# Whole-matrix loads on two queues and a transpose by DMA, in an eight-core attention and FFN layer kernel

## The reference

```python
def attn(x, bind_key, unbind_key, gate, decay):        # x: [8, 2048, 1024]
    bound = circ_conv(x, bind_key)
    d = sigmoid(decay)
    decay_matrix = where(t >= s, d ** (t - s), 0)
    hologram = einsum('ts,bsd->btd', decay_matrix, bound)
    return x + gate * circ_corr(hologram, unbind_key)

def ffn(x, w_gate, w_up, w_down):                      # int weights / 127, hidden 3072
    h = silu(x @ wg.T) * (x @ wu.T)
    return h @ wd.T

x = x + layernorm(attn(layernorm(x)))
x = x + layernorm(ffn(layernorm(x)))
```

## Time and profile before

| | us |
|---|---|
| median of 2 runs | 831.39 (831.27 to 831.5) |
| profiled execution, whole time | 832.75 |
| profiled execution, span of the slowest core | 831.2 |
| spans of the 8 cores | 818.4 to 831.2 |
| PE busy in the span | 679.4 |
| DVE busy, ACT busy | 248.8, 208.2 |

### The profile page before, as it was taken

The page is one execution under the profiler, slowest core; times in us unless marked ns, Lnnn a source line. Parts: engine busy times, 40 slices in busy tenths (PEclk is TensorE's granted clock), DMA queues, the critical chain, the costliest instruction groups (busy, mean ns, idle before and its releaser), DMA issues.

```text
span 831.2 us, 8438 instructions; the slowest of 8 cores (818.4 to 831.2 us)
## 1 busy us (share of the span) xinstructions
PE 679.4 (82%) x3030; PEld 300.2 (36%) x3030; DVE 248.8 (30%) x595; ACT 208.2 (25%) x309; POOL 40.7 (5%) x80
## 2 busy tenths in 40 slices
PE   0538489999700699799999999699999999999994
PEld 0113222343300344344444444343444444444441
DVE  0532431055557212612121123233111111112333
ACT  2001422244341421211111132423111111112222
POOL 7000000000000000000000000000000000000000
PEclk9878765699955599899999999789999999999998
DMA  7999500000002034434444201013444444400111
GB/s 176 237 259 165 93 1 0 1 1 0 1 0 51 1 53 76 76 52 76 76 77 76 50 26 52 25 44 84 76 76 76 77 76 76 76 1 26 51 52 76
DMA packets 13145, 53.40 MB, mean 64 GB/s; under 512 B 1472, under 2 KB 1472, under 8 KB 12848
## 3 DMA queue, kind: packets, MB, share of 16 engines
q0 software_dynamic: 10800, 44.47, 28.7%
q1 hardware_dynamic: 2304, 8.39, 2.5%
HBM read 80.12 MB, written 8.39 MB: 106 GB/s over the span
## 4 chain that ended last, share of the span: by engine, by line
PE 71%; DVE 9%; issue 6%; ACT 6%; DMA 5%; POOL 2%; DVEq 0%; ACTq 0%; POOLq 0%
PE pg L642 20%; PE pu L650 19%; PE pu L719 10%; PE pf L719 10%; DMA x<-xin 5%; PE pb L364 4%; PE cp L239 3%; ACT t1a L439 2%; DVE sqd L418 2%; PE pt L579 2%; ACT t1a L411 2%; PE pb L359 1%; DVE sta L544 1%; DVE x2t L583 1%; PE pr L481 1%
## 5 line engine op out<-in xcount | busy, mean ns | idle before, releaser
L642 PE MATMUL pg<-x2t,wgu 128*128 128x512 bf16 x768 | 178.6, 387 | 9.5 <-DVE xw L669 6.9
L650 PE MATMUL pu<-x2t,wgu 128*128 128x512 bf16 x768 | 173.6, 379 | 0.0
L663 ACT ACTIVATE sil<-pg,z 128x512 bf16<-128x512 f32 x96 | 65.5, 687 | 241.0 <-PE pg L642 240.9
L642 PEld LDWEIGHTS pg<-x2t,wgu 128*128 128x128 bf16 x768 | 76.0, 99 | 104.7 <-issue 18.0
L650 PEld LDWEIGHTS pu<-x2t,wgu 128*128 128x128 bf16 x768 | 75.1, 98 | 90.6
L669 DVE SCALAR_TENSOR_TENSOR xw<-sil,pu 128x512 bf16<-128x512 bf16 x64 | 43.7, 688 | 167.9 <-PE pu L650 165.8
L239 PE MATMUL cp<-cubb,cbtb 128*128 128x512 bf16 x128 | 38.3, 471 | 46.2 <-DMA x<-xin 43.8
L481 PE MATMUL pr<-hc,zt 128*128 128x512 bf16 x256 | 63.1, 391 | 7.5 <-ACT t1a L411 6.6
L719 PE MATMUL pf<-wdtb,xw 128*128 128x512 bf16 x256 | 57.9, 379 | 2.1 <-DVE hc L669 2.1
L719 PE MATMUL pu<-wdtb,xw 128*128 128x512 bf16 x256 | 59.5, 387 | 0.0
L64 POOL DMA_DIRECT2D wgu<-wgu x48 | 25.4, 530 | 679.8 <-PE pu L650 441.9
(11 more groups left out here) (94 smaller groups left out, 450.5 us busy)
## 6 DMA issues: line engine op xcount, KB each, us to landing
wgu<-wgu POOLq DMA_DIRECT2D x48, 512.0 KB, 5.1
x<-xin POOLq DMA_DIRECT2D x16, 512.0 KB, 28.5
out<-x SPq DMA_DIRECT2D x16, 512.0 KB, 2.7
wdtb<-wdt POOLq DMA_DIRECT2D x1, 6144.0 KB, 81.1
cbtb<-cbt POOLq DMA_DIRECT2D x4, 512.0 KB, 23.3
cubb<-cuT POOLq DMA_DIRECT2D x4, 512.0 KB, 25.5
cstf_s<-cstf POOLq DMA_DIRECT2D x1, 257.0 KB, 3.3
cstb_s<-cstb POOLq DMA_DIRECT2D x1, 128.0 KB, 2.9
```

What stands on the lines that cost most here:

```text
L642: pe_g[eta][c] = op("tensor", lambda e, sl=sl, c=c, d=d: e.matmul(PG[sl][:, 512 * c:512 * c + 512], WGU[sl][:, 128 * d:128 * d + 128], X2T ...
L650: pe_u[eta][c] = op("tensor", lambda e, sl=sl, c=c, d=d: e.matmul(PU[sl][:, 512 * c:512 * c + 512], WGU[sl][:, 1024 + 128 * d:1024 + 128 * ...
L663: sc_sil[eta][c] = op("scalar", lambda e, sl=sl, c=c: e.activation(SIL[sl][:, 512 * c:512 * c + 512], PG[sl][:, 512 * c:512 * c + 512], AF ...
```

## The change

Three things change. First, the X tiles are loaded from SP, each 512 KB without a cast, at the very start; POOL loads the two circulants whole, one DMA each, and issues WDTB only after all X tiles have landed. Second, the circulant product waits for both circulants, then goes block by block through 4 PSUM banks, with the contraction index on the inside. Third, X2T is filled by a DMA transpose from SP in place of PE, PT and the DVE copy: ACT's tile tl waits for the transpose of tile tl - 2 (semaphores XA0, XA1, XB0, XB1), and the gate matmuls wait for the last two transposes.

```diff
+    for t in range(TN):
+        dma("sync", X[t][:], xin[:, 1024 * t:1024 * t + 1024], f"LDX{t // 4 + 1}".replace("LDX1", "LDX"))
-    for q in range(4):
-        gsem = f"LDX{q + 1}".replace("LDX1", "LDX")
-        dma("gpsimd", CBTB[:, 2048 * q:2048 * q + 2048], cbt[:, 2048 * q:2048 * q + 2048], gsem)
-        dma("gpsimd", CUBB[:, 2048 * q:2048 * q + 2048], cuT[:, 2048 * q:2048 * q + 2048], gsem)
-        for t in range(4 * q, 4 * q + 4):
-            dma("gpsimd", X[t][:], xin[:, 1024 * t:1024 * t + 1024], gsem)
+    dma("gpsimd", CBTB[:], cbt[:, :], "WCC")
+    wt_ccin = dma("gpsimd", CUBB[:], cuT[:, :], "WCC")
+    for gname in ("LDX", "LDX2", "LDX3", "LDX4"):
+        w("gpsimd", gname, 64)
     wt_wd = dma("gpsimd", WDTB[:], wdt[:, :], "WWD")
...
-    CP = [pa.enter_context(nc.psum_tensor(f"cp{i}", [128, 512], F32)) for i in range(8)]
+    CP = [pa.enter_context(nc.psum_tensor(f"cp{i}", [128, 512], F32)) for i in range(4)]
+    w("tensor", "WCC", wt_ccin)
-    for half in range(2):
-        g0 = 8 * half
-        if half == 1:
-            w("tensor", "SC", dv_ccevac[7])
+    for g in range(16):
+        dj, fc = g // 2, g % 2
+        if g >= 4:
+            w("tensor", "SC", dv_ccevac[g - 4])
         for k in range(ND):
...
-            w("scalar", "PE", pe_tr[tl - 2] if tl >= 2 else prev_pe_tr[tl - 2])
+            if tl >= 2:
+                w("scalar", f"X{HN}{tl % 2}", xt[tl - 2])
+            elif prev_xt is not None:
+                w("scalar", f"XA{tl % 2}", prev_xt[tl + 6])
             sc_x2[tl] = op("scalar", lambda e, t=t, tl=tl: e.activation(
                 X2S[tl % 2][:], X[t][:], AF.Identity,
                 bias=NB2s[:, t:t + 1], scale=R2s[:, t:t + 1]), "SC")
-            for d in range(ND):
-                pe_tr[tl] = op("tensor", lambda e, tl=tl, d=d: e.transpose(
-                    PT[:, 128 * d:128 * d + 128], X2S[tl % 2][:, 128 * d:128 * d + 128], IDB[:]),
-                    "PE" if d == ND - 1 else None)
-            w("vector", "PE", pe_tr[tl])
-            dv_pt[tl] = op("vector", lambda e, tl=tl: e.tensor_copy(...), "DV")
+            w("sync", "SC", sc_x2[tl])
+            if tl == 0:
+                w("sync", "PE", pe_before)
+            sem = f"X{HN}{tl % 2}"
+            plan["sync"].append(lambda e, tl=tl, s=sem: e.dma_start_transpose(
+                X2T[:, :].rearrange("p (d t) -> p d t", d=ND)[:, :, 128 * tl:128 * tl + 128],
+                X2S[tl % 2][:, :].rearrange("p (d t) -> p d t", d=ND)).then_inc(S[s], 16))
```

More of the change, by code:

```diff
@@ L40, in build_nc @@
     C = {"LDX": 0, "LDX2": 0, "LDX3": 0, "LDX4": 0, "LDC": 0, "WCC": 0, "WWD": 0,
-         "WG0": 0, "WG1": 0, "PE": 0, "DV": 0, "SC": 0, "GP": 0, "ST": 0}
+         "WG0": 0, "WG1": 0, "XA0": 0, "XA1": 0, "XB0": 0, "XB1": 0,
+         "PE": 0, "DV": 0, "SC": 0, "GP": 0, "ST": 0}
     S = {}
@@ L170, in finish_debug @@
         w("sync", "PE", C["PE"])
-        for snm in ("WCC", "WWD", "WG0", "WG1"):
+        for snm in ("WCC", "WWD", "WG0", "WG1", "XA0", "XA1", "XB0", "XB1"):
             w("sync", snm, C[snm])
@@ L228, in build_nc @@
     last_chain_end = {0: 0, 1: 0}
-    for half in range(2):
-        g0 = 8 * half
-        if half == 1:
-            w("tensor", "SC", dv_ccevac[7])
+    for g in range(16):
+        dj, fc = g // 2, g % 2
+        if g >= 4:
+            w("tensor", "SC", dv_ccevac[g - 4])
         for k in range(ND):
[L234 to L250, removed]
+            pe_cc[g] = op("tensor", lambda e, dj=dj, fc=fc, k=k, g=g:
+                          e.matmul(CP[g % 4][:], CBTB[:, 1024 * k + 128 * dj:1024 * k + 128 * dj + 128],
+                                   CUBB[:, 1024 * k + 512 * fc:1024 * k + 512 * fc + 512],
+                                   start=(k == 0), stop=(k == ND - 1)),
+                          "PE" if k == ND - 1 else None)
+        w("scalar", "PE", pe_cc[g])
+        dv_ccevac[g] = op("scalar", lambda e, dj=dj, fc=fc, g=g:
+                          e.activation(HC[dj][:, 512 * fc:512 * fc + 512], CP[g % 4][:],
+                                       AF.Identity, bias=0.0, scale=1.0), "SC")
         if phases <= 0.77:
             continue
+        t = g
         if t % 4 == 0:
-            w("vector", f"LDX{t // 4 + 1}".replace("LDX1", "LDX"), 96)
+            w("vector", f"LDX{t // 4 + 1}".replace("LDX1", "LDX"), 64)
         p = 12 * (t % 2)
@@ L557, in emit_ln2, with emit_x2pipe @@
         return ln_combine(tg0, 8, M1c, R2s, NB2s, fold=INV127)
-    def emit_x2pipe(hf, dv_ln2, psum_sc, psum_dv, prev_pe_tr):
+    def emit_x2pipe(hf, dv_ln2, pe_before, prev_xt):
         tg0 = 8 * hf
-        PT = ffps["PT"]
         sc_x2 = [0] * 8
-        pe_tr = [0] * 8
-        dv_pt = [0] * 8
+        xt = [0] * 8
+        HN = "B" if hf else "A"
         for tl in range(8):
@@ L571, in emit_x2pipe @@
                 bias=NB2s[:, t:t + 1], scale=R2s[:, t:t + 1]), "SC")
-            w("tensor", "SC", sc_x2[tl])
+            w("sync", "SC", sc_x2[tl])
             if tl == 0:
[L574 to L577, removed]
-            for d in range(ND):
-                pe_tr[tl] = op("tensor", lambda e, tl=tl, d=d: e.transpose(
-                    PT[:, 128 * d:128 * d + 128], X2S[tl % 2][:, 128 * d:128 * d + 128], IDB[:]),
-                    "PE" if d == ND - 1 else None)
-            w("vector", "PE", pe_tr[tl])
[L583 to L590, removed]
+                w("sync", "PE", pe_before)
+            sem = f"X{HN}{tl % 2}"
+            C[sem] += 16
+            xt[tl] = C[sem]
+            plan["sync"].append(lambda e, tl=tl, s=sem: e.dma_start_transpose(
+                X2T[:, :].rearrange("p (d t) -> p d t", d=ND)[:, :, 128 * tl:128 * tl + 128],
+                X2S[tl % 2][:, :].rearrange("p (d t) -> p d t", d=ND)).then_inc(S[s], 16))
+        return sc_x2, xt
     dv_ln2_done = 0
@@ L599, in build_nc @@
             dv_ln2_done = emit_ln2(0, 0)
+            _warm_done = True
             for wv in (stat_fin[1], stat_fin[3], stat_fin[5], stat_fin[7],
@@ L605, in build_nc @@
                     start=True, stop=True, skip_group_check=True))
-            sc_x2, pe_tr, dv_pt = emit_x2pipe(0, dv_ln2_done, prev_half_sc, prev_half_dv,
-                                              [pe_retr[15]] * 2)
+            sc_x2, xt_cnt = emit_x2pipe(0, dv_ln2_done, pe_retr[15], None)
         else:
-            sc_x2, pe_tr, dv_pt = x2pipe_B
+            sc_x2, xt_cnt = x2pipe_B
         if phases <= 4:
@@ L635, in build_nc @@
             w("tensor", f"WG{sl}", wt_gu[eta])
-            w("tensor", "DV", dv_pt[7])
+            if eta < 2:
+                hn = "B" if hf else "A"
+                w("tensor", f"X{hn}0", xt_cnt[6])
+                w("tensor", f"X{hn}1", xt_cnt[7])
             if eta >= 2:
@@ L730, in build_nc @@
             if hf == 0 and tl == 5:
-                x2pipe_B = emit_x2pipe(1, dv_ln2_done, sc_cpf[4], 0, pe_tr)
+                x2pipe_B = emit_x2pipe(1, dv_ln2_done, pe_u[NH - 1][1], xt_cnt)
         sc_sqf[7] = dn_stage2(7)
```

## The result

The changed kernel takes 811.19 us (median of 11 executions) where the kernel before, run on the same chip, takes 833.44 (10 executions). The ratio is 0.9726, with a 95% interval of 0.9712 to 0.9739: 2.7% faster, where the forecast was 843 us, slower. Executions in which some cores ran at a visibly lower clock than the others (five of the 11 after the change) are left out of every ratio here.

The account below looks back on a forecast made before the run. It took the loads before the scan and the transposes of halves A and B as the places that change: -21 + 24.0 + 8.2 = +11.2 us on 832.75, 844.0, which lies 1.36 above the median, so 843 us; range 803 to 888.

Parts of the forecast that it names:

- The price of a short run: DMA transposes: each 256-byte run costs 0.075 us, so 4.8 us per tile and 6.2 us from issue to landing.
- rival (a): Transposes: fast, 0.01 us per run, 2.0 us to landing, two buffers set the pace; 796 us in all; chance 0.2.
- Half A: From half A's first x2s to its first gate matmul: 41.3 us with DMA transposes against 17.25, +24.0 us.
- Half B: Half B's transpose: the stall moves from PE to ACT's queue, gate product +5.9 us, with PE's slow start +8.2 us.
- cold start: Half B's gate product: PE idle beforehand, so its first 16 matmuls lose 2.3 us.
- The loads: Start to scan: engines alternate queues by packet, circulants land at 35.4 us, scan starts at 74.1; -21 us taken.
- the dearer packet: Circulant loads: at 0.49 us per 4 KB, the circulants land at 40.9 us and the gain is 16 us.
- (b): Loads: queues share by bytes or SP's goes first, circulants land last, scan +1.0 us; 865 us in all; chance 0.25.
- (c): Transposes: slow, 0.12 us per run, 9.1 us to landing, one per 7.7 us; 884 us in all; chance 0.2.

Follow-up runs that it names:

- short_packets: The changed kernel with each circulant loaded in four DMAs of 2048 columns, so packets of 4 KB in place of 16 KB: 820.96 us, ratio 0.9861.
- four_buffers: The changed kernel with four buffers for x2s in place of two, the two SIL buffers being lent: 797.07 us, ratio 0.9571.
- spread_x2s: The changed kernel with half B's eight x2s issued two at a time behind the third to sixth down tiles' copies, not all behind the sixth: 801.26 us, ratio 0.9637.
- one_queue: The changed kernel with X issued from POOL behind the circulants and WDTB behind X, without the wait: 806.39 us, ratio 0.9696.
- wdt_early: The changed kernel without POOL's wait for the X tiles ahead of the down weights (WDTB): 843.37 us, ratio 1.013.

## Why the prediction was wrong

**The price of a short run (the step that failed).** The forecast took 0.075 us for each 256-byte run, past the middle towards the 0.12 us of a packet of the cast loads, "since short packets are the nearer row". The runs are packets of their own, as assumed, but cost 0.021 us each. The moving part of a tile is 1.37 us and not 4.8, and a transpose lands after 3.2 us and not 6.2. The 0.11 us per packet came from cast loads out of HBM on POOL's queue; nothing in the trace said that it held for an SBUF to SBUF transfer without a cast on SP's, and here it didn't. The runs don't bear it out for cast loads either: 62.1% x 16 us x 16 / 475 = 0.335 us for a packet of 3.6 KB in `short_packets` and 1.41 us for one of 14.5 KB in the changed kernel are 0.092 and 0.097 us per KB, which leaves nothing for the packet itself. The 0.11 had come out of one stretch of 2 us. With short runs this cheap the pace comes from the buffers, as in rival (a): x2s 1.35 us, landing 3.2, so some 4.7 us per pair (253.06, 257.81, 262.44 in the chain). Half A came out at +2.7 where the forecast had +24.0 and rival (a), with 2.0 us to landing, -2.3. `four_buffers` shows that it is the buffers: with twice as many, the same transposes take 5.7 us less.

Two places of the Trainium skill, named in the prediction against each other, can be set beside this. The Trainium skill's Advanced Engine Details and Errata, X-Bar Transpose (TRN2), has transposing DMAs as fast as plain ones. The trace agrees half way: some 200 GB/s in the humps above, half the 410 of a store alone, and 3.2 us to landing for 256 KB against 2.6 to 2.7 for the 512 KB of a store. The Trainium skill's other place, VectorE: DVE Perf Modes, The three transpose paths, gives 1309 ns for one 128x128 block by DMA. The trace doesn't bear out multiplying it: eight blocks in one DMA landed in 3.2 us, not in 10.5.

**Half B.** The mechanism was right: the stall moved from PE to ACT's queue, PE goes on after the sixth tile, and the gate product starts 543.18 - 531.30 = 11.9 us behind the end of the last x2s (forecast 12.8). Only the time of the x2s was off, by the same price: the eighth ends 16.3 us after the first starts, where 32.9 was forecast. So -11.6 in place of +5.9. The 2.3 us of cold start were 2.8. `spread_x2s` confirms it by taking the queue away.

**The loads.** The mechanism was right (turns by packet, `short_packets`), and the size was 4 us off: -16.8 against -21. The forecast circulant packet of 1.62 us and X packet of 0.2 us measured 89.4% x 14 us x 16 / 142 = 1.41 us and 0.22 us, so a turn was even shorter. What was late was the start, for which the forecast had 2 us from issue and 1 us to landing without a row. The three small loads of constants stand on POOL's queue ahead of the circulants and now share with X packets; they landed 8.3, 8.8 and 9.0 us after issue, where it was 3.3, 2.9 and 3.7; in `one_queue`, with no X packets beside them, it is 3.4, 3.0 and 4.1. The last of them landed at 2.79 + 9.0 = 11.8 us, and 16 turns of 1.63 us counted back from 39 us begin at 13, where 5.3 was assumed. That the dearer packet's end, 40.9 us, met the measured 40.05 was chance. The rest went as forecast: 29.57 us of product (forecast 29.4), 8.57 to the scan, and X's statistics end (L281 starts at 65.6) ahead of the last copy.

**The rest of the sum.** Rival (a)'s 796.2 us, with the loads at -16.8 (+4.2), half A at +2.7 (+5.0), half B at -8.8 instead of -11.9 (+3.1), and +1.4 for two stages in which nothing was forecast, comes to 809.9 us, and with the 1.36 us that were subtracted for the profiled execution 811.3; 811.19 was measured. Of the 1.4 us, +1.9 lies in half A's gate and up products; 1.1 of it are two waits for gate and up weights (0.49 us before 295.03 and 0.64 before 381.21) that core 2 didn't have before. Of the other cores only core 4 has such waits in this stage, of 0.32 and 0.52 us, and before the change core 4 had one of 1.32 in half B's. Where they come from was not tried and stays open. The table is that of core 2: on six of the other seven cores half B's gate and up products take 169.0 to 169.3 us after the change, 0.5 to 1.2 more than on the same core before, and not 2.8 more.

**Rivals (b) and (c).** In (b) the circulants would have landed last, near 58; they landed at 40 while X landed at 58.4. In (c) a transpose would have taken 9.1 us to landing; it took 3.2.

## What to carry to other kernels

The price of a packet read from one kind of transfer (cast, from HBM, on one queue) is no price for another kind; where the two ends of a bound are twelve times apart and decide the sign, the middle is no forecast but a gap in the evidence. Two queues on the same DMA engines took turns by packet here, so the one with the longer rows got the bytes: give the long rows to what is needed first, and hold back a long-row load that is needed last. One queue in the order of need did it too, and 4.8 us better. When a wait for PE becomes a wait for a DMA of some 3 us, look at the buffers in front of it and at what stands behind the waiting instruction on its engine; four buffers in place of two, or the queue spread out, gave 14 and 10 us more here.

## What the runs showed of the hardware

SP's issue of a transpose takes 1.23 to 1.34 us of SP's time, about the engines' 1.37 us per transpose. SP's issue of plain loads was held back while much was in flight: the sixteen X loads took 28.8 us to issue in `short_packets`, 38.5 in the changed kernel and 76.0 in `wdt_early`. The timeline of the changed kernel:

```profile
1.06 38.52 SPq L65 DMA_DIRECT2D x<-xin  x16
```

That of `wdt_early`:

```profile
1.06 76.01 SPq L65 DMA_DIRECT2D x<-xin  x16
```

The spread among the cores, 789.6 to 809.7 us after the change, arises mostly in the scan and goes with the granted clock. Stretches of the changed kernel on core 2, 79 to 124 us, in which it is in the scan (its length, busy time and count of PE, PEld, DVE, ACT and POOL, then the clock):

```profile
79.00:124.00 45.00, 40.38 (x136) 13.95 (x134) 12.00 (x18) 14.22 (x24) 0.00 (x0) 0.63 0.38 62
```

The same stretch on core 7, which is in the scan too:

```profile
79.00:124.00 45.00, 39.09 (x176) 15.38 (x176) 12.95 (x19) 18.35 (x32) 0.00 (x0) 0.85 0.46 77
```

Both cores change between 2.4 and 1.2 GHz (four matmuls of the scan take 0.72 us at the one and 1.25 at the other), but core 7 has the higher clock for longer: it runs 176 matmuls where core 2 runs 136, and ends the scan at 124.75 where core 2 ends it at 138.96. Their first x2s of half A follow at 235.60 and 251.69. Ahead of it both did the same work, the same product and then some 9 us without a matmul; why the clock fell for longer on one core was not tried.
